# Routing divided in two halves and the shared expert begun on the first half's norm, in a fused ViT tower kernel

## The chip, the cores and the metric

The kernel runs on one core of a Trainium2 chip. The metric is the device time of one execution in microseconds. The kernel before was run three times: 373.65, 376.08 and 376.28 us.

## What is computed

16 images of 96x96 pixels become 36 patch tokens each and one class token: 592 tokens of width 256. Then come two blocks. The reference, cut to the block that the change touches:

```python
h = tok(x, ...)                                   # (16, 37, 256)
h = h + attn(layernorm(h), ...)                   # 16 heads of 64, relative bias, softmax
h = h + ffn(layernorm(h), ...)                    # below
h = h + scan_attn(layernorm(h), ...)              # second block
h = h + channel_mix(layernorm(h), ...)
...
def ffn(x, router_w, w_gate, w_up, w_down, sw_gate, sw_up, sw_down):
    logits = x_flat @ router_w.T                  # 7 experts
    top_vals, top_idx = top_k(logits, 2)
    top_w = softmax(top_vals)
    combine = sum(one_hot(top_idx, 7) * top_w[..., None], axis=1)
    routed_out = swiglu(x_flat, w_gate, w_up, w_down)      # hidden width 1024
    mixed = einsum("end,ne->nd", routed_out, combine)
    shared_out = swiglu(x_flat, sw_gate, sw_up, sw_down)   # one shared expert
    return mixed + mean(shared_out, axis=0)
```

All of it is float32. The kernel makes each float32 product as three products of a high and a low part (`three`): high x high, high x low, low x high.

## The kernel before

The state `hT` lies transposed in SBUF: two blocks `m` of 128 channels by 592 tokens. The tokens are cut into two halves `c` of 296 columns. TensorE (PE) makes the products, ScalarE (ACT) the activations and the high parts (`piece_high`, `high`, `shared_high`), VectorE (DVE) the gate products and most low parts (`sub` at L859, called by `piece_low`, `low` and `shared_low`), GpSimd (POOL) the remaining low parts of weights (`half_low` L386, `down_low` L391) and the scatters, SyncE (SP) the loads. Each engine has its program written out by hand, in one block for each; the order in the code is the order on the engine, and semaphores tie the engines together. The weights of an expert come in five pieces: gate and up in halves `g0`, `u0`, `g1`, `u1`, and `dn`. Expert 0 is the shared one, 1 to 7 the routed ones.

Layer norm of a half is a chain over three engines: `mean` (PE, L1362, two float32 products with a matrix of ones), `centre` (DVE, L891), `square` (ACT, L536), `variance` (PE, L1369), `root` (ACT, L541 and L543: logarithm and exponential), `normal` (DVE, L896), `high` (ACT, L547), `low` (DVE, L859). The order around the change is this.

- PE ends the attention's output projection (`output`, with the first half's mean and variance between its products), then makes the second half's mean and variance, and then begins the shared expert. ACT and DVE make in that time the high and low parts of the shared expert's weights, POOL the low parts of `u1` and `dn`.
- The shared expert runs over 12 units `u` here (the last 4 come behind the routed experts). A unit is one block of 128 hidden channels for one half: 12 products of 296 columns (`gate_up`), Silu on ACT (L639), the gate product on DVE (L1074), high part on ACT (L646), low part on DVE, and two units later six down products on PE (`down`). Units 0 to 7 belong to the first half, 8 to 11 to the second.
- Routing lies between the units. `logits` (PE, L1542) stands behind unit 1 and waits for the second half's norm. `rank_experts` (DVE) compares the seven logits of every token of five tiles of 128 tokens pair by pair. `positions` (PE, L1565) gives each token its place in its expert's list: for each tile one triangular product and products with ones for all tiles before it, 20 in all. `rows` turns places into row numbers. `turn_tokens` (PE, L1555) turns the normed tokens, `tokens_copy` (ACT, L653) takes them over, and POOL scatters each tile twice by row number into `expert_rows` in DRAM (L425, ten scatters). SP waits for all of them and loads the rows of expert 1 (L346) and of the others (L348). `turn_rows(1)` in unit 11 turns expert 1's rows for PE.
- In unit 6 ACT makes the exponentials of the shifted logits (L666), which `token_weights` (DVE) turns into weights. The exponential and Silu lie in different tables, so the engine loads one table ahead of it (ACT_TABLE_LOAD, L666) and the other behind it (L639).
- Then the seven routed experts follow, each with 256 gathered rows, some 18.5 us each by the chain.

## Time and profile before

| | us |
|---|---|
| three runs: lowest, median, highest | 373.65, 376.08, 376.28 |
| profiled execution, its own time | 373.84 |
| profiled execution, span of the core | 371.6 |
| PE busy in the span | 334.2 (90%) |
| DVE, ACT, POOL busy | 209.7, 194.0, 152.6 |

The rows below come from this one profiled execution. Times are microseconds from the start of the span. The span runs from the first to the last instruction; the execution's own time is 2.2 us longer. The granted clock is a share of TensorE's full 2.4 GHz.

### The profile page before, as it was taken

How to read it: one execution, taken by the hardware profiler on the slowest of the kernel's cores; microseconds unless marked ns; L12 is line 12 of the kernel's file. 1: busy time of each engine (PE TensorE's matmuls, PEld its weight loads, DVE VectorE, ACT ScalarE, POOL GpSimd, SP SyncE). 2: the span in 40 equal slices, each digit the busy share in tenths (PEclk: the TensorE clock that was granted, in tenths of full speed). 3: DMA queues.
4: the chain of work that ended last, by engine and by line, in shares of the span. 5: the costliest groups of instructions: out<-in, count | busy, mean ns of one | idle time of the engine just before them, and what ended most of it. 6: DMA issues, size and time to landing. Idle time of an engine off the chain costs nothing.

```text
span 371.6 us, 7692 instructions
## 1 busy us (share of the span) xinstructions
PE 334.2 (90%) x3284; PEld 309.9 (83%) x3284; DVE 209.7 (56%) x347; ACT 194.0 (52%) x322; POOL 152.6 (41%) x103
## 2 busy tenths in 40 slices
PE   7979999999999599779999999999999969578794
PEld 6957877899989399779999999999999969457694
DVE  2773233566536853155757574747474764637586
ACT  4662233756536633446566666666666554245491
POOL 3050021674422503732646464646464888100031
PEclk9998999999999799969999999999999998879899
DMA  8836440003002520282664656464648232100001
GB/s 294 342 113 192 118 178 2 4 10 109 4 2 78 191 89 28 101 268 71 198 199 165 211 163 207 161 220 155 207 163 284 85 113 59 30 3 0 2 1 65
DMA packets 31426, 45.40 MB, mean 122 GB/s; under 512 B 1714, under 2 KB 20226, under 8 KB 31260
## 3 DMA queue, kind: packets, MB, share of 16 engines
q1 hardware_dynamic: 28140, 39.84, 32.2%
q0 software_dynamic: 1200, 3.03, 2.7%
q10 hardware_dynamic: 2048, 1.99, 1.8%
q8 instruction: 27, 0.44, 0.5%
q14 instruction: 11, 0.09, 0.1%
HBM read 38.80 MB, written 5.88 MB: 120 GB/s over the span
## 4 chain that ended last, share of the span: by engine, by line
PE 73%; DVE 10%; ACT 6%; issue 5%; DMA 2%; another core or an unknown queue 1%; SPq 1%; POOL 0%; DVEq 0%; ACTq 0%
PE ps L1337 21%; PE ps L1339 19%; PE ps L1338 19%; PE ps L1468 2%; PE ps L1495 2%; PE ps L1369 2%; DMA w_stage<-in_w_v 2%; PE ps L1362 2%; DVE xn_lo L859 2%; DVE c_region L859 2%; PE ps L1453 1%; DVE w_lo L859 1%; DVE x_centred L891 1%; DVE v_region L1269 1%
## 5 line engine op out<-in xcount | busy, mean ns | idle before, releaser
L1337 PE MATMUL ps<-c_region,w_hi 128*128 128x256 f32 (+2 forms) x320 | 95.0, 297 | 7.6 <-DVE c_region L859 7.2
L1338 PE MATMUL ps<-c_region,w_hi 128*128 128x256 f32 (+2 forms) x320 | 92.3, 289 | 0.0
L1339 PE MATMUL ps<-c_region,w_lo 128*128 128x256 f32 (+2 forms) x320 | 92.3, 288 | 0.0
L386 POOL TENSOR_TENSOR w_lo<-w_stage,w_hi 128x1024 fp32r<-128x1024 f32 x16 | 47.7, 2981 | 58.3 <-ACT w_hi L619 58.3
L1337 PEld LDWEIGHTS ps<-c_region,w_hi 128*128 128x128 f32 x320 | 61.5, 192 | 9.6 <-DVE c_region L859 8.9
L1338 PEld LDWEIGHTS ps<-c_region,w_hi 128*128 128x128 f32 x320 | 61.5, 192 | 0.1
L1339 PEld LDWEIGHTS ps<-c_region,w_lo 128*128 128x128 f32 x320 | 61.4, 192 | 0.0
L859 DVE TENSOR_TENSOR c_region<-s_region,c_region 128x512 fp32r<-128x512 f32 (+1 forms) x44 | 49.0, 1114 | 16.1 <-ACT c_region L743 15.4
L1337 PE MATMUL ps<-xn_hi,w_hi 128*128 128x296 f32 x152 | 49.3, 324 | 6.1 <-issue 3.4
L619 ACT ACTIVATE w_hi<-w_stage 128x1024 fp32r<-128x1024 f32 (+1 forms) x43 | 51.6, 1209 | 4.1 <-DVE v_region L1189 3.4
L1338 PE MATMUL ps<-xn_lo,w_hi 128*128 128x296 f32 x152 | 47.2, 310 | 0.0
L1339 PE MATMUL ps<-xn_hi,w_lo 128*128 128x296 f32 x152 | 47.1, 310 | 0.0
L391 POOL TENSOR_TENSOR w_lo<-w_stage,w_hi 128x2048 fp32r<-128x2048 f32 (+1 forms) x9 | 39.3, 4371 | 13.5 <-ACT w_hi L619 11.5
L1337 PEld LDWEIGHTS ps<-xn_hi,w_hi 128*128 128x128 f32 x152 | 30.6, 201 | 7.4 <-issue 7.2
L1337 PE MATMUL ps<-w_hi,c_region 128*128 128x256 f32 x112 | 32.1, 287 | 3.5 <-issue 3.5
L403 POOL TENSOR_TENSOR s_region<-s_region,softmax_stats 101x296 f32<-101x296 f32 x16 | 11.1, 692 | 52.0 <-DVE softmax_stats L941 52.0
L1338 PE MATMUL ps<-w_lo,c_region 128*128 128x256 f32 x112 | 31.7, 283 | 0.0
L1339 PE MATMUL ps<-w_hi,c_region 128*128 128x256 f32 x112 | 31.7, 283 | 0.0
L1159 DVE TENSOR_TENSOR s_region<-s_region,ps 128x512 f32<-128x512 f32 x28 | 19.0, 679 | 21.2 <-ACT s_region L738 21.2
L743 ACT ACTIVATE c_region<-s_region 128x512 fp32r<-128x512 f32 x28 | 17.7, 633 | 24.8 <-DVE s_region L1159 22.9
L1338 PEld LDWEIGHTS ps<-xn_lo,w_hi 128*128 128x128 f32 x152 | 30.6, 201 | 0.0
L1339 PEld LDWEIGHTS ps<-xn_hi,w_lo 128*128 128x128 f32 x152 | 30.4, 200 | 0.0
(164 smaller groups left out, 621.7 us busy)
## 6 DMA issues: line engine op xcount, KB each, us to landing
w_stage<-in_w_gate SPq DMA_DIRECT2D x17, 512.0 KB, 3.8
w_stage<-in_w_up SPq DMA_DIRECT2D x17, 512.0 KB, 4.5
w_stage<-in_w_down SPq DMA_DIRECT2D x8, 1024.0 KB
expert_rows<-zeros SPq DMA_DIRECT2D x1, 1792.0 KB, 14.1
expert_out<-v_region ACTq DMA_DIRECT2D x7, 256.0 KB, 4.8
v_region<-in_patches SPq DMA_DIRECT2D x3, 576.0 KB, 6.0
v_region<-expert_rows SPq DMA_DIRECT2D x1, 1536.0 KB, 7.5
v_region<-in_w_l SPq DMA_DIRECT2D x1, 1280.0 KB, 6.9
```

Source lines behind the costliest of these rows:

```text
L386: g.tensor_tensor(piece(wl, n), piece(ws, n), piece(wh, n).bitcast(F32), ALU.subtract).then_inc(lo_e[n], 1)
L391: g.tensor_tensor(piece(wl, "dn", rows), piece(ws, "dn", rows), piece(wh, "dn", rows).bitcast(F32), ALU.subtract).then_inc(lo_e["dn"], 1)
L403: g.tensor_tensor(sc, sc, pat(stat[0:QR, :], (t % 3) * 24, [1, 8], [0, T]), ALU.subtract).then_inc(s["shifted"], 1)
L619: a.activation(piece(wh, n, rows), piece(ws, n, rows), ACT.Copy).then_inc(hi_e[n], 1)
L743: a.activation(gh_h[:, i * G:(i + 1) * G], prod_g[:, (i % 2) * G:(i % 2 + 1) * G], ACT.Copy).then_inc(s["g_hi"], 1)
L859: return v.tensor_tensor(o, x, hi.bitcast(F32), ALU.subtract)
L1159: v.tensor_tensor(pat(prod_g, (i % 2) * G, [SLOTS, 2], [1, SLOTS]), pat(silu_g, (i % 2) * G, [SLOTS, 2], [1, SLOTS]), pat(bank(2 * (i % 2) ...
L1337: mm(o, a_h, b_h, start=start, stop=False)
L1338: mm(o, a_h, b_l, start=False, stop=False)
L1339: return mm(o, a_l, b_h, start=False, stop=stop)
L1362: w = mm(bank(2 * c, NC), ones[:], hT[:, k * N + c * NC:k * N + (c + 1) * NC], start=(k == 0), stop=(k == KD - 1))
L1369: w = mm(bank(var_bank(L, c), NC), ones[:], sq[:, k * N + c * NC:k * N + (c + 1) * NC], start=(k == 0), stop=(k == KD - 1))
```

## The change

It does the following.

- Routing is divided: tiles 0 and 1 (`TA` = 2, all in the first half) and tiles 2 to 4. Each part has its logits, ranking, positions and rows. The two parts use PSUM banks 7 and 6.
- The shared expert's first unit needs only the first half's norm. The second half's mean stands behind unit 0 on PE, its variance behind unit 1, its square, root and high part in units 0, 1 and 2 on ACT, its other steps in units 0 to 2 on DVE. Between `root` and the next Silu ACT switches tables twice.
- Positions are two float32 products for each part: the triangular matrix gives the place inside a tile, the matrix of ones each tile's total. DVE copies the totals into a small table and scans it (`tensor_tensor_scan`) for the first place of each tile.
- The exponentials for the weights move from unit 6 to the end of expert 1, `token_weights` and `choice_weights` to expert 2.
- The shared down weights are made in two halves, high on ACT, low on DVE; POOL makes the low parts of `u0` and of `u1`, the second half of `u1` after unit 0's gate product.
- The third turning of tokens uses the bank of the second and waits for its copy (`xt_ok` 2).
- The routing constants become columns of `const` (277 to 622 columns); their own load on ACT's queue goes. SP loads `u0` ahead of `g1`.

The core of the diff:

```diff
@@ block.sync
             load("g0", 0)
-            load("g1", 0)
             sp.wait_ge(w_lo[1], 1)
             sp.wait_ge(s["up_lo"], 1)
             load("u0", 0)
+            load("g1", 0)
             load("u1", 0)
@@ block.gpsimd
-            half_low("u1", 0)
-            down_low(0)
-            pool.wait_ge(s["d_zero"], 16)
-            pool.wait_ge(s["rows_set"], 1)
+            half_low("u0", 0)
+            pool.wait_ge(hi_e["u1"], 1)
+            for k in range(KD):
+                if k == 1:
+                    pool.wait_ge(s["gate_mul"], 1)
+                r = slice(W1 + k * HID + HID // 2, W1 + (k + 1) * HID)
+                w = g.tensor_tensor(wl[:, r], ws[:, r], wh[:, r].bitcast(F32), ALU.subtract)
+            w.then_inc(lo_e["u1"], 1)
+            pool.wait_ge(s["d_zero"], 48)
             for t in range(TT):
+                pool.wait_ge(s["rows_set"], 1 if t < TA else 2)
                 pool.wait_ge(s["xt_ok"], (1, 1, 2, 2, 3)[t])
@@ block.scalar
-            piece_high("g0", 0)
-            piece_high("g1", 0)
+            for n in ("g0", "u0", "u1", "g1"):
+                piece_high(n, 0)
             square(1, 0)
-            piece_high("u0", 0)
-            piece_high("u1", 0)
             root(1, 0)
+            high(1, 0)
+            preload(ACT.Silu, 7)
             act.wait_ge(s["wo_mm"], 4)
-            piece_high("dn", 0)
-            high(1, 0)
-            square(1, 1)
-            root(1, 1)
-            preload(ACT.Silu, 7)
+            shared_down_high(0, s["dn0_hi"])
...
             for u in range(FRONT):
                 silu(0, u)
                 if u == 0:
+                    shared_high(0)
+                    square(1, 1)
+                    tokens_copy(0)
+                if u == 1:
+                    log_exp_tables()
+                    root(1, 1)
+                    shared_high(1)
+                    preload(ACT.Silu, 7)
+                if u == 2:
                     high(1, 1)
-                if u >= 1:
-                    shared_high(u - 1)
-                if u in (2, 3, 5):
-                    tokens_copy((2, 3, 5).index(u))
-                if u == 6:
-                    act.wait_ge(s["rt_shift"], 1)
-                    a.activation(route[:, 80:115], route[:, 80:115], ACT.Exp).then_inc(s["rt_exp"], 1)
+                    shared_down_high(1, hi_e["dn"])
+                if u >= 2:
+                    shared_high(u)
+                if u in (5, 6):
+                    tokens_copy(u - 4)
...
+                    if e == 1:
+                        weight_exponentials()
                     act.wait_ge(s["g_y"], e)
@@ block.vector
             add_attention(0)
             add_attention(1)
+            piece_low("g0", 0)
             centre(1, 0)
-            piece_low("g0", 0)
+            add_attention(2)
             piece_low("g1", 0)
-            piece_low("u0", 0)
-            add_attention(2)
-            add_attention(3)
             normal(1, 0)
-            centre(1, 1)
             low(1, 0)
...
+            def rows(i, t0, t1):
...
+                dve.wait_ge(s["pos_mm"], i)
+                link(v.tensor_copy(pat(tot, 1 + t0, [1, n], [TT + 1, E]),
+                                   pat(bank(route_bank(t0)), TOT0 + t0 * 8, [8, n], [1, E])))
+                link(v.tensor_tensor_scan(first, rcb[:, RB_KEEP:RB], tot, 0.0, ALU.mult, ALU.add))
...
+            take_logits(1, 0, TA)
+            add_attention(3)
+            rank_experts(0, TA)
             for u in range(FRONT):
...
                 if u == 0:
+                    centre(1, 1)
+                    shared_down_low(0, s["dn0_hi"], s["dn0_lo"])
+                if u == 1:
+                    shared_low(0)
+                    rows(1, 0, TA)
+                    normal(1, 1)
+                    shared_low(1)
+                if u == 2:
                     low(1, 1)
-                if u >= 1:
-                    shared_low(u - 1)
-                if u == 1:
-                    rank_experts()
+                if u == 5:
+                    rows(2, TA, TT)
+                if u >= 2:
+                    shared_low(u)
+                if u == 3:
+                    take_logits(2, TA, TT)
+                    rank_experts(TA, TT)
+                if u == 4:
+                    shared_down_low(1, hi_e["dn"], lo_e["dn"])
@@ block.tensor
-            output(1, 1, 0, HP // 2)
+            output(1, 1, 0, 1)
             variance(1, 0)
-            output(1, 1, HP // 2, HP)
-            mean(1, 1)
-            variance(1, 1)
+            output(1, 1, 1, HP)
...
-            def positions():
-
-                pe.wait_ge(s["sel_set"], 2)
-                for t in range(TT + 1):
-                    o = bank(6, 8, POS0 + t * 8) if t < TT else bank(6, 8, CNT0)
-                    for j in range(min(t + 1, TT)):
-                        w = mm(o, tri_r if j == t else one_r, sel_r[:, j * 8:(j + 1) * 8],
-                               start=(j == 0), stop=(j == min(t, TT - 1)))
+            def positions(t0, t1, chosen):
+
+                pe.wait_ge(s["sel_set"], chosen)
+                b, r = route_bank(t0), slice(t0 * 8, t1 * 8)
+                for o, c_ in ((POS0, RB_TRI), (TOT0, RB_ONES)):
+                    w = mm(bank(b, (t1 - t0) * 8, o + t0 * 8), rcb[:, c_:c_ + P], sel[:, r], start=True, stop=True)
                 w.then_inc(s["pos_mm"], 1)
...
+            logits(0, TA, 3)
             half_ready(0, 0)
             pe.wait_ge(s["ln_lo"], 3)
             gate_up(0, 0)
+            mean(1, 1)
+            turn_tokens(0)
             gate_up(0, 1)
-            logits()
+            positions(0, TA, 2)
+            variance(1, 1)
```

**What the order shows.** Three places are given, of the kernel before and of the changed one apart. A row is one instruction or several alike (x3), with the tensor that it writes, the tensors that it reads, its size and the semaphores that it waits for.

PE, from the last product of the attention's output projection to the shared expert's first, before:

```order
L1339 MATMUL ps<-c_region,w_lo 128x296
L1362 MATMUL ps<-hT,ones_over_d 128x296 [waits h_ready]
L1362 MATMUL ps<-hT,ones_over_d 128x296
L1369 MATMUL ps<-x_squared,ones_over_d 128x296 [waits ln_sq]
L1369 MATMUL ps<-x_squared,ones_over_d 128x296
L1337 MATMUL ps<-xn_hi,w_hi 128x296 [waits ln_lo,lo_u0,lo_g0]
```

and in the changed kernel:

```order
L1400 MATMUL ps<-c_region,w_lo 128x296
L1601 MATMUL ps<-params,xn_f 128x7 [waits ln_xn]
L1601 MATMUL ps<-params,xn_f 128x7 x3
L1398 MATMUL ps<-xn_hi,w_hi 128x296 [waits ln_lo,lo_u0,lo_g0]
L1399 MATMUL ps<-xn_lo,w_hi 128x296
```

The second half's mean and variance have left this place, and four logit products (tiles 0 and 1) stand there.

ACT, units 6 and 7 of the shared expert before, with the exponential (`s_region` 128x35) between two table loads:

```order
L646 ACTIVATE c_region<-s_region 128x296 [waits dn_mm,gate_mul]
L666 ACT_TABLE_LOAD
L666 ACTIVATE s_region<-s_region 128x35 [waits rt_shift]
L639 ACT_TABLE_LOAD [waits gate_mul]
L639 ACTIVATE s_region<-ps 128x296 [waits gu_mm]
```

and units 1 and 2 in the changed kernel:

```order
L655 ACTIVATE s_region<-ps 128x296 [waits gu_mm]
L527 ACT_TABLE_LOAD
L557 ACTIVATE rstd<-ps,eps 128x296 [waits ln_var]
L559 ACTIVATE rstd<-rstd 128x296 [waits ln_log]
L662 ACTIVATE c_region<-s_region 128x296 [waits gate_mul]
L548 ACT_TABLE_LOAD
L548 ACTIVATE small<-eps 128x1
L655 ACTIVATE s_region<-ps 128x296 [waits gate_mul,gu_mm]
```

The pair of table loads in the shared expert now encloses the second half's root, ahead of unit 2; the exponential's pair is in experts 1 and 2.

DVE, from the end of the rows (`count_i`) to unit 5's gate product and low part, before:

```order
L1044 CAST count_i<-v_region 128x1
L1074 TENSOR_TENSOR s_region<-s_region,ps 128x296 [waits hid_lo,hid_hi,silu_ok]
L859 TENSOR_TENSOR c_region<-s_region,c_region 128x296 [waits hid_hi]
L1074 TENSOR_TENSOR s_region<-s_region,ps 128x296 [waits hid_lo,hid_hi,silu_ok]
L859 TENSOR_TENSOR c_region<-s_region,c_region 128x296 [waits dn_mm,hid_hi]
```

and from the end of the second ranking to unit 5's gate product in the changed kernel:

```order
L1043 TENSOR_REDUCE s_region<-s_region 128x21 [waits dve_chain]
L1044 TENSOR_SCALAR s_region<-s_region 128x21 [waits dve_chain]
L1045 TENSOR_TENSOR s_region<-s_region,consts 128x3x7 [waits dve_chain]
L1120 TENSOR_TENSOR s_region<-s_region,ps 128x296 [waits hid_lo,hid_hi,silu_ok]
L889 TENSOR_TENSOR c_region<-s_region,c_region 128x296 [waits dn_mm,hid_hi]
L889 TENSOR_TENSOR w_lo<-w_stage,w_hi 128x1024 [waits hi_dn]
L1120 TENSOR_TENSOR s_region<-s_region,ps 128x296 [waits hid_lo,hid_hi,silu_ok]
```

Between unit 3 and unit 5 DVE now has the ranking of tiles 2 to 4 and half of the down weights' low part.

## Rows read from the trace of the kernel before

**Rows 1.** The stretches by engine (us; busy and count; granted clock; DMA).

```profile
125.00:131.40 6.40, 4.46 (x15) 3.49 (x15) 4.28 (x5) 2.44 (x4) 2.56 (x1) 0.50 0.41 131
...
158.70:165.60 6.90, 5.25 (x21) 5.25 (x22) 3.45 (x10) 3.70 (x8) 2.87 (x1) 0.52 0.85 276
```

**Rows 2.** Chain that ended last, first norm half to shared expert (start, us, what).

```profile
120.88 0.15 PE ps L1339
121.06 0.48 DVE hT L968
121.58 1.28 PE ps L1362 x4
...
128.33 0.58 PE ps L1337
```

**Rows 3.** Timeline of DVE over the same stretch.

```profile
123.59 4.60 DVE L859 TENSOR_TENSOR xn_lo<-xn_f,xn_hi 128x592 fp32r<-128x592 f32 x1
```

**Rows 4.** Timeline of POOL, weight low part and last scatter.

```profile
123.05 4.51 POOL L391 TENSOR_TENSOR w_lo<-w_stage,w_hi 128x2048 fp32r<-128x2048 f32 x1 [1.45 <-ACT w_hi L619]
...
156.32 0.91 POOL L425 DMA_INDIRECT expert_rows<-v_region,row_i  x1 [0.30 <-issue]
```

**Rows 5.** Chain that ended last, the pause in the shared expert.

```profile
153.18 1.28 ACT L639
154.47 4.51 another core or an unknown queue
...
159.83 0.47 DVE c_region L859
...
160.96 0.25 PE ps L1338
```

**Rows 6.** Timeline of SP, first load behind the scatters.

```profile
158.63 0.37 SPq L346 DMA_DIRECT2D v_region<-expert_rows  x1
```

**Rows 7.** Timeline of PE, an f32 pair of products inside the output projection.

```profile
113.98 1.16 PE L1362 MATMUL ps<-hT,ones_over_d 128*128 128x296 f32 x4
114.75 0.52 PE L1337 MATMUL ps<-c_region,w_hi 128*128 128x296 f32 x1
```

**Rows 8.** Chain that ended last, logits and positions.

```profile
133.53 2.40 PE ps L1542 x20
...
140.57 2.13 PE ps L1565 x20
```

**Rows 9.** Timeline of ACT, switch back to Silu.

```profile
127.44 1.28 ACT L532 ACT_TABLE_LOAD   x1
128.73 0.20 ACT L532 ACTIVATE small<-eps 128x1 f32<-128x1 f32 x1
```

**Rows 10.** DVE groups by form between 100 and 175 us (busy, mean ns).

```profile
L859 DVE TENSOR_TENSOR w_lo<-w_stage,w_hi 128x1024 fp32r<-128x1024 f32 x5 | 5.9, 1221 | 0.2 <-ACT w_hi L619 0.2
...
L1006 DVE TENSOR_TENSOR s_region<-s_region 128x245 f32<-128x245 f32 x1 | 0.4, 416 | 0.0
...
L1013 DVE TENSOR_TENSOR c_region<-s_region,v_region 128x35 fp32r<-128x35 f32 x1 | 0.2, 196 | 0.0
```

**Rows 11.** Timeline of PE, seventh unit, end of the second pause, turning of gathered rows.

```profile
148.95 0.38 PE L1337 MATMUL ps<-xn_hi,w_hi 128*128 128x296 f32 x1
...
160.35 0.61 PE L1337 MATMUL ps<-c_region,w_hi 128*128 128x296 f32 x1 [4.62 <-DVE c_region L859]
...
170.25 0.60 PE L1579 MATMUL ps<-consts,v_region 128*128 128x128 f32 x4
```

**Rows 12.** DMA issues: KB each, median us to landing.

```profile
v_region<-expert_rows SPq DMA_DIRECT2D x1, 256.0 KB, 2.8
consts<-in_const SPq DMA_DIRECT2D x1, 138.5 KB, 6.6
```

**Rows 13.** Page, part 2: GB/s in 40 slices of 9.3 us.

```profile
GB/s 294 342 113 192 118 178 2 4 10 109 4 2 78 191 89 28 101 268 71 198 199 165 211 163 207 161 220 155 207 163 284 85 113 59 30 3 0 2 1 65
```

**Rows 14.** Chain that ended last, at the start.

```profile
5.45 7.96 DMA w_stage<-in_w_v
```

202 lines of the change are left out of this document (116 added, 86 removed).

## The prediction

> **What bounds the kernel now.** I read the page first. TensorE (PE) is busy 90% of the span, so time can only be won where PE stands still, where it runs at the lower clock, or where it does work that can be left out. The second view was the row of granted clocks and then the stretches by engine: between 125 and 131.4 us and between 158.7 and 165.6 us the granted clock is 0.50 and 0.52, that is 1.2 GHz where the neighbours have 2.4 [rows 1]. Both stretches lie in the part that the change rewrites, the norm before the expert stage and the shared expert, and each follows a pause of PE. The third view was the chain of waits around both.
>
> First pause: the last product of the attention output ends at about 121.0, the second half's mean follows at 121.58, and the first product of the shared expert starts at 128.33 [rows 2]. What it waits for is DVE's low part of the first half's norm: a 128x592 subtraction that took 4.60 us [rows 3]. POOL worked on a 128x2048 weight low part from 123.05 to 127.56 [rows 4], and the subtraction ended 0.6 us after that. So DVE's subtraction of two SBUF operands stood still behind POOL's.
>
> Second pause: ACT loads the Silu table at 153.18 after the routing's exponential, and its next instruction starts only at 159.0 [rows 5]; PE resumes at 160.35 after 4.62 us without work [rows 11]. The profile names no engine for these 4.51 us. They end just where the last scatter has landed: the load that waits for all scatters is issued at 158.63 [rows 6]. Behind each pause the products are 0.25 us apart [rows 5] where they were 0.15 apart before it [rows 2].
>
> **The change part by part.** All times are on the axis of the profiled execution (span 371.6, own time 373.84).
>
> (a) First pause. The shared expert no longer waits for the second half. Its inputs are the first half's norm and the low parts of g0 and u0. The first half's own variance stands nine products earlier, so ACT's root can start some 1.3 us earlier. POOL now has u0 (from ACT's second high part, about 113.7, for 2.9 us) and half of u1, and the down weights have left it; it waits at u1's second half until unit 0's gate product. So no POOL work lies beside DVE's low part of the norm, which should take 0.8 and be done by about 121.7. PE meanwhile does the logits of tiles 0 and 1: 4 of 10 products, 20 records in 2.40 [rows 8], so 8 records of 0.12, 1.0 us. The first shared product starts at about 122.1 instead of 128.33: 6.2 us. If DVE's g1 low part falls behind POOL's u1 piece, it ends about 119.4 and the norm still comes in time; without that cover the price would be some 1 us.
>
> (b) The lower clock behind it. The first unit's 12 products ran 0.25 apart instead of 0.14: 12 x 0.11 = 1.3 us.
>
> (c) PE's own work. The remaining 12 logit records cost 1.4 in the place of 2.4: 1.0 us. The positions, 20 records in 2.13 [rows 8], become two f32 products in each half. No row shows this form; the nearest is the logits, an f32 call with two records, so 8 records of 0.12: 1.0 us, saving 1.2. Bounds: four records (0.5) and, if the 16 or 24 columns cost as the f32 products of 296 do (0.77 for two, [rows 7]), 1.6. Against this, the second half's mean and variance are now between products. A mean of this kind holds the next product up by 0.77, which is itself 0.1 to 0.2 slower [rows 7]: 1.0 each, together minus 2.0.
>
> (d) A new wait. The third turning of tokens now uses the bank of the second and waits for ACT's copy of it. That copy stands behind unit 5's gate on ACT, and this behind a queue on DVE: after unit 3 come the take-over and ranking of tiles 2 to 4 (five operations between 0.20 and 0.42, [rows 10], so about 0.35 each, and three of 0.2: 2.4 us), unit 4's two operations, and 1.2 for the second half of the down weights [rows 10], then unit 5. Followed, unit 5's gate product ends at 141.5, the copy at 142.5, and PE arrives at 140.6. That is 2.0 us; bounds are 0 (the handshakes overlap better) and 4 (each of some ten handshakes is 0.2 longer). Queued behind PE's waiting instruction is unit 6, and nobody else waits. The clock fell in the trace behind pauses of more than twice that; I leave it at the upper level and take 2.0.
>
> From (a) to (d): 6.2 + 1.3 + 1.0 + 1.2 - 2.0 - 2.0 = 5.7 us. Unit 6, at 148.95 before [rows 11], should start at about 143.2.
>
> (e) Second pause. The exponential and the switch back to Silu have left the shared expert. If the pause goes with them, PE gains its 4.6 us [rows 11], and the 21 products to 165.6 that ran at half clock, 21 x 0.11 = 2.3: 6.9 us. What is late next is the gathered rows. The scatters of tiles 0 and 1 start at about 130.5, well covered. The other six wait for the rows of the second half, about 143.1 in my hand trace; at 0.91 + 0.30 each [rows 4] they end at 150.6, land by 152, and the load takes 2.8 [rows 12]: 154.9. PE turns these rows at 170.25 before [rows 11], now at 157.6. Slack 2.7 us. The whole cover is that; if the scatters start 4 us later, 1.3 is lost.
>
> (f) The exponential in expert 1 stands on ACT where it waits for the expert's down products anyway. The switch back delays expert 2's first Silu by 1.28 [rows 9]; PE wants the product of that Silu only after the 24 products of its second step. Nothing, bounds 0 and 1.3. Token weights on DVE have the same kind of cover: nothing.
>
> (g) The start. The constants grow from 277 to 622 columns, 138.5 KB [rows 12] to 311, ahead of w_v, whose load ends the wait at 13.4 us and is on the chain [rows 14]. 172 KB at the 294 to 342 GB/s of the first slices [rows 13] are 0.5 to 0.6 us, at most; I take minus 0.5. The routing constants' own load behind the attention goes, hidden before.
>
> Sum: 5.7 + 6.9 - 0.5 = 12.1; 373.84 - 12.1 = 361.7. The three runs have a median of 376.08, 2.24 above the profiled execution. I carry a quarter, 0.6, since a pause that varies would be the first thing to differ between runs and it is among what goes: 362.3.
>
> A rule of the Trainium skill speaks against the three added switches. Here the row is first: the table load at 127.44 took 1.28 and the activation stands right behind it, at 128.73 [rows 9]. ScalarE: Activation LUTs, section What ACT_TABLE_LOAD costs, adds about 1.38 us of drain to each load. By that rule unit 1's two switches make ACT 2.8 us later, which the new wait of (d) passes on: 364.5 plus 0.6. It is a rival below, priced there by rows.
>
> **The rivals.**
>
> R1, the pause stays. ACT would not be held by the table but by something that the scatters hold, and it is freed when they land. For: it ends with them [rows 5, 6], and the switch at 127.44, with no scatter under way, had none [rows 9]. Against: ACT ran on through the first scatters, and only the instruction behind a switch was held. In the changed kernel ACT at unit 7 (147.2) would stand until about 152.0; PE has work to 150.4 and resumes at about 153: 2.6, plus 2.3 for the clock: 4.9. 362.3 + 4.9 = 367.2.
>
> R2, ACT's switches cost more than their 1.28 (a drain, or longer handshakes on ACT and DVE): up to 2.8 more at unit 1, passed on in full by (d): 365.1. For: the long hand-over at 154.47. Against: 128.73. The skill's drain would be this case.
>
> R3, slower. Every switch back to Silu has the pause of the second one: 4.6 and 2.3 of clock, 6.9 us. There are now three (before unit 0, in unit 1, before expert 2). It decides from two on: 362.3 + 13.8 = 376.1, and with three 383.0. Against: of two such switches in the trace one had no pause.
>
> R4, the first half cannot start early: DVE's g1 low part and the norm behind it stand behind POOL's u0 and u1 pieces (as [rows 3, 4] show for another pair), and the chain of ACT and DVE in units 0 to 2 starves PE for the 5.7 us of (a) to (d). Then only the second pause goes: 362.3 + 5.7 = 368.0. Against: the wait for unit 0's gate product keeps POOL off most of it.
>
> **How the numbers follow.** My forecast 0.62, R1 0.18, R2 0.08, R4 0.08, R3 0.04. The forecast's own spread is the bounds of (c), (d) and (e), about 359 to 365, and up to 2.2 for the offset of the median. R1, R2 and R4 reach 368. Range 358 to 368. A measurement of this kernel tells about 1% from no change, 3.8 us: below 372.3 is faster. All cases but R3 are below it; two of its switches end as no change, three as slower. With a little for what I have not seen: faster 0.93, same 0.04, slower 0.03.
>
> **What would show it.** Right: the first shared product about 1 us after the attention output; the low part of the norm under 1 us; no clock of 0.5 between 120 and 160; a short wait of PE at the turning of two tiles behind unit 5; the load behind the scatters issued near 152; expert 1 about 12 us earlier. (e) falls if ACT shows one idle time of several us without an engine's name while scatters run. (a) falls if a DVE subtraction of several us stands before unit 0. A total above 370 would mean that both gains were given back.

## The result and the profile after

The changed kernel took 364.03 us (median of five runs, 363.31 to 365.81), the kernel before, run beside it, 375.86 (five runs). The ratio is 0.973, with a 95% interval from 0.969 to 0.976: faster. Here and below a ratio leaves out executions over 1.5% slower than the fastest of their kernel, a median does not. The forecast was 362.3 with a range of 358 to 368. The profiled execution is the slowest of the five: its own time is 365.81, its span 363.8. From its page, the engines' totals and the row of granted clocks in 40 slices of 9.1 us:

```profile
PE 332.2 (91%) x3272; PEld 307.1 (84%) x3272; DVE 214.3 (59%) x366; ACT 196.5 (54%) x326; POOL 150.4 (41%) x104
...
PEclk9988999999999999999999999999999989769898
```

The two stretches at lower clock of [rows 1], around 125 and 160 us, are gone; what is left stands at the start and in the tail. The timeline of PE, at the places that the prediction spoke of (start, duration, idle time before and what ended it):

```profile
122.58 0.30 PE L1400 MATMUL ps<-c_region,w_lo 128*128 128x296 f32 x1
122.71 0.95 PE L1601 MATMUL ps<-params,xn_f 128*128 128x7 f32 x8
123.54 0.37 PE L1398 MATMUL ps<-xn_hi,w_hi 128*128 128x296 f32 x1
...
128.67 1.24 PE L1430 MATMUL ps<-x_squared,ones_over_d 128*128 128x296 f32 x4
129.53 0.52 PE L1398 MATMUL ps<-xn_hi,w_hi 128*128 128x296 f32 x1
...
143.27 0.44 PE L1614 MATMUL ps<-consts,xn_f 128*128 128x128 f32 x2 [1.34 <-ACT v_region L669]
143.46 0.38 PE L1398 MATMUL ps<-xn_hi,w_hi 128*128 128x296 f32 x1
...
158.72 0.63 PE L1636 MATMUL ps<-consts,v_region 128*128 128x128 f32 x4 [0.77 <-DVE s_region L1120]
...
161.72 0.40 PE L1398 MATMUL ps<-c_region,w_hi 128*128 128x296 f32 x1 [0.69 <-DVE c_region L889]
```

The row at 122.71 (the first eight logit records) stands right behind the attention's last product, which starts at 122.58; the first shared product follows at 123.54, 0.96 behind the attention's last. Before, that distance was 7.61: the first shared product started at 128.33 [rows 2] and the attention's last one here:

```profile
120.72 0.30 PE L1339 MATMUL ps<-c_region,w_lo 128*128 128x296 f32 x1
```

The second half's variance (128.67) holds up the next product until 129.53. PE waits 1.34 at the third turning, and 0.77 and 0.69 in units 10 and 11. It never stands for the 4.6 us of [rows 11].

The norm's low part on DVE, and the second table load on ACT with the activation behind it:

```profile
122.61 0.78 DVE L889 TENSOR_TENSOR xn_lo<-xn_f,xn_hi 128x592 fp32r<-128x592 f32 x1 [0.76 <-ACT xn_hi L563]
```

```profile
128.94 1.28 ACT L527 ACT_TABLE_LOAD   x1
130.24 0.51 ACT L557 ACTIVATE rstd<-ps,eps 128x296 f32<-128x296 f32 x1
```

The subtraction takes 0.78 us instead of the 4.60 of [rows 3]. The switch takes 1.28, as in [rows 9], and the activation stands right behind it. Now ACT around the last scatters (POOL issues the last one at 150.25), and SP's load that waits for all of them:

```profile
149.15 1.04 ACT L633 ACTIVATE w_hi<-w_stage 128x1024 fp32r<-128x1024 f32 x1
152.59 0.42 ACT L655 ACTIVATE s_region<-ps 128x296 f32<-128x296 f32 x1 [2.39 <-remote]
```

```profile
152.55 0.37 SPq L357 DMA_DIRECT2D v_region<-expert_rows  x1
```

This is the row that the prediction named as evidence against its term (e). ACT's Silu of unit 8 starts at 152.59 after 2.39 us without work, no engine is named, no table is loaded there, and it starts when the scatters have landed (152.55), as in [rows 5, 6]. PE had ended unit 8 at about 150.3.

Two places give time back. One is expert 2. The rows of PE are the first down product of experts 1, 2 and 3 (175.68, 194.20, 214.76) and a wait ahead of the third; then the same three products before:

```profile
175.68 0.35 PE L1398 MATMUL ps<-w_hi,c_region 128*128 128x256 f32 x1 [0.64 <-issue]
...
194.20 0.35 PE L1398 MATMUL ps<-w_hi,c_region 128*128 128x256 f32 x1 [0.59 <-issue]
...
210.99 0.39 PE L1398 MATMUL ps<-c_region,w_hi 128*128 128x256 f32 x1 [1.45 <-DVE s_region L1212]
...
214.76 0.35 PE L1398 MATMUL ps<-w_hi,c_region 128*128 128x256 f32 x1 [0.64 <-issue]
```

```profile
186.37 0.35 PE L1337 MATMUL ps<-w_hi,c_region 128*128 128x256 f32 x1 [0.64 <-issue]
...
204.86 0.36 PE L1337 MATMUL ps<-w_hi,c_region 128*128 128x256 f32 x1 [0.57 <-issue]
...
223.36 0.36 PE L1337 MATMUL ps<-w_hi,c_region 128*128 128x256 f32 x1 [0.57 <-issue]
```

Before, they are 18.5 apart; after, 18.52 and then 20.56, with a wait of 1.45 for DVE's gate product between them. The other is the clock at the start. Stretches by engine of the changed kernel (granted clock is the column behind POOL):

```profile
core 0: us, PE busy (x) PEld busy (x) DVE busy (x) ACT busy (x) POOL busy (x), PEclk, DMA share, GB/s
19.00:21.00 2.00, 0.47 (x1) 0.50 (x2) 2.00 (x5) 1.18 (x1) 2.00 (x1) 0.83 0.76 201
21.00:23.00 2.00, 2.00 (x5) 1.35 (x4) 0.35 (x2) 0.73 (x1) 1.93 (x2) 0.50 0.91 322
23.00:25.00 2.00, 1.82 (x6) 1.01 (x5) 1.27 (x2) 0.70 (x1) 1.16 (x1) 0.82 0.00 1
```

Before, the clock was 1.00 there and fell to 0.66 at 28 to 32 us. In this execution it fell twice: again at 28 to 36 us, to 0.82 and 0.75. The first fall is common: of the ten profiles of the changed kernel and its variants it stands in seven, and not in `weights_early`, `exp_in_unit6` and `all_three`; of the four of the kernel before and its variants in one (`before_copy_for_exp`). Whether the change makes it more frequent, so few profiles don't show. The changed kernel's repetition and its variants without added products have the attention's last product at 120.07 to 121.25 us, this one at 122.58 and the kernel before at 120.72: most of the loss at the start belongs to the single execution.

The balance of the two profiled executions, by PE's rows: minus 1.86 at the end of the attention (0.35 of it the later start on w_v), plus 7.35 to unit 6 (28.23 us before, 20.88 after, counted from the attention's last product), plus 5.20 from there to expert 1's start (37.42 and 32.22), minus 2.06 in expert 2, minus about 0.9 in the tail, at lower clock (0.66 in the 15 us from 310, 0.77 in the 15 from 319 before). That is 7.7 of the spans' difference of 7.8.

### The profile page after: what moved, and what is told of

The parts are those of the page before. It is cut to its first block, busy times and chain, and to the rows that moved or that the text cites. A ratio compares the mean times of both kernels' runs of the same rounds, so it can differ in the third digit from the quotient of the medians.

```text
span 363.8 us, 7696 instructions
## 1 busy us (share of the span) xinstructions
PE 332.2 (91%) x3272; PEld 307.1 (84%) x3272; DVE 214.3 (59%) x366; ACT 196.5 (54%) x326; POOL 150.4 (41%) x104
## 4 chain that ended last, share of the span: by engine, by line
PE 62%; DVE 16%; ACT 10%; issue 7%; DMA 2%; SPq 1%; another core or an unknown queue 1%; ACTq 0%; POOL 0%; DVEq 0%
PE ps L1398 17%; PE ps L1400 15%; PE ps L1399 15%; DVE c_region L889 4%; PE ps L1423 3%; PE ps L1430 2%; PE ps L1529 2%; PE ps L1556 2%; DMA w_stage<-in_w_v 2%; DVE w_lo L889 2%; DVE s_region L1212 1%; PE ps L1514 1%; ACT w_hi L633 1%; ACT L548 1%; ACT c_region L770 1%
## 5 line engine op out<-in xcount | busy, mean ns | idle before, releaser
L633 ACT ACTIVATE w_hi<-w_stage 128x1024 fp32r<-128x1024 f32 (+1 forms) x42 | 49.6, 1192 | 5.5 <-DVE v_region L1246 5.5
L1398 PE MATMUL ps<-xn_hi,w_hi 128*128 128x296 f32 x152 | 48.1, 316 | 4.1 <-issue 3.3
L1399 PE MATMUL ps<-xn_lo,w_hi 128*128 128x296 f32 x152 | 46.0, 303 | 0.0
L1400 PE MATMUL ps<-xn_hi,w_lo 128*128 128x296 f32 x152 | 45.9, 302 | 0.0
L402 POOL TENSOR_TENSOR w_lo<-w_stage,w_hi 128x2048 fp32r<-128x2048 f32 (+1 forms) x8 | 34.8, 4348 | 14.1 <-ACT w_hi L633 14.1
L1398 PEld LDWEIGHTS ps<-xn_hi,w_hi 128*128 128x128 f32 x152 | 29.4, 193 | 4.9 <-issue 4.4
L889 DVE TENSOR_TENSOR w_lo<-w_stage,w_hi 128x1024 fp32r<-128x1024 f32 (+1 forms) x22 | 28.8, 1307 | 2.7 <-ACT w_hi L532 2.4
L1399 PEld LDWEIGHTS ps<-xn_lo,w_hi 128*128 128x128 f32 x152 | 29.3, 192 | 0.1
```

Source lines behind the costliest of these rows:

```text
L402: g.tensor_tensor(piece(wl, "dn", rows), piece(ws, "dn", rows), piece(wh, "dn", rows).bitcast(F32), ALU.subtract).then_inc(lo_e["dn"], 1)
L633: a.activation(piece(wh, n, rows), piece(ws, n, rows), ACT.Copy).then_inc(hi_e[n], 1)
L889: return v.tensor_tensor(o, x, hi.bitcast(F32), ALU.subtract)
L1398: mm(o, a_h, b_h, start=start, stop=False)
L1399: mm(o, a_h, b_l, start=False, stop=False)
L1400: return mm(o, a_l, b_h, start=False, stop=stop)
```

## The experiments

Three theories were open. T: a table switch is held while scatters run (the prediction's). S or C: something of the scatters holds the units' hand-over, with or without a switch. F, formed after the first four runs: PE's instruction packets among the scatters are the cause. Beside these, the loss in expert 2 and the terms (a), (d) and (g) were tested one at a time. Times of different groups were not taken side by side; the ratio to the kernel before, run beside them, is the safer number. Of a single profile, the distances between two of PE's rows tell more than the total, since the clock at the start and in the tail differs from one execution to the next.

### The changed kernel once more

> The changed kernel as it is, beside the three others of this job, so that they are compared on one chip. Expected: 364.0 us within 1 us; if the 1.5 us that the profiled execution lost to a lower clock at 20 to 25 us is a matter of the single execution, this profile has the first mean at 2.3 us for 8 records instead of 3.8.

365.02 us (362.76 to 365.35), ratio 0.974 [0.968, 0.981]. The first mean's eight records took 3.53, so the clock fell early here too, against what I expected. It did not fall a second time, and the attention's last product stands at 120.94. PE's waits are the same: 1.34, 0.19, 0.77, 0.69, and 1.43 in expert 2.

### Where the token weights stand

```diff
-                    if e == 2:
-                        token_weights()
-                        dve.wait_ge(s["comb_set"], 2)
-                        choice_weights()
                     dve.wait_ge(s["g_y"], e)
...
                     v.tensor_copy(y_s[:, o:o + D], bank(5, D)).then_inc(s["y_ok"], 1)
+                    if e == 1:
+                        token_weights()
+                        dve.wait_ge(s["comb_set"], 2)
+                        choice_weights()
```

> Only the place of the token weights on DVE changes: from ahead of expert 2's output copy to behind expert 1's, where DVE stands idle from 182.1 to 186.5 and POOL until 184.6. Theory: expert 2 is 20.56 us long instead of 18.5 because a 128x35 product took 2.40 us beside POOL's 128x1024 low part and the output copy, the next expert's down weights and the first gate product stand behind it; then expert 2 falls to 18.5, the time by 2.06 to 362.0, and the product takes 0.2. Rival: the loss is the switch back to Silu (1.28) at the head of expert 2; then expert 2 stays above 20 us and the time at 364.

360.08 us (358.83 to 362.61), ratio 0.965 [0.958, 0.972]. The reading starts with the changed kernel's chain of waits in expert 2 and POOL's row beside its first line:

```profile
198.81 2.33 DVE s_region L1055
...
202.40 0.34 DVE v_region L1246
...
203.18 1.92 ACT w_hi L633
...
207.00 3.34 DVE c_region L889
...
210.99 0.39 PE ps L1398
```

```profile
197.98 3.10 POOL L397 TENSOR_TENSOR w_lo<-w_stage,w_hi 128x1024 fp32r<-128x1024 f32 x1 [2.84 <-ACT w_hi L633]
```

A product of 35 columns held DVE for 2.33 us, until POOL's subtraction ended at 201.1 (the row itself is 2.40 long). Behind it stood the output copy, behind that ACT's high part of the down weights (203.18), then Silu and the gate product, and at 207.00 DVE was held once more, for 3.34, by POOL's next piece. PE got the result at 210.99. With the weights moved:

```profile
179.63 0.57 DVE L1055 TENSOR_TENSOR s_region<-s_region 128x35 f32<-128x35 f32 x1
```

```profile
191.79 0.36 PE L1398 MATMUL ps<-w_hi,c_region 128*128 128x256 f32 x1 [0.59 <-issue]
...
210.27 0.36 PE L1398 MATMUL ps<-w_hi,c_region 128*128 128x256 f32 x1 [0.55 <-issue]
```

The product takes 0.57, and from expert 2's first down product to expert 3's it is 18.48. The table load at its head is still there, so the rival (the switch) is out; `exp_in_unit6` below shows the same from the other side, with no table load there and still 20.57. The median is 4.9 us below the run above, and 2.06 of them are this edit. The profiles differ besides by 0.9 at unit 6, ahead of the edit, and by 3.5 behind expert 7's first down product, with a mean granted clock of 0.987 here and 0.971 above.

### The exponentials back in unit 6

```diff
                 if u in (5, 6):
                     tokens_copy(u - 4)
+                if u == 6:
+                    act.wait_ge(s["rt_shift"], 1)
+                    a.activation(ex, ex, ACT.Exp).then_inc(s["rt_exp"], 1)
...
-                    if e == 1:
-                        weight_exponentials()
```

> The exponentials go back to unit 6 of the shared expert on ACT, with their two table loads, all else as changed. Theory T (a table switch under way while scatters run is held until they have landed): ACT's Silu of unit 7 starts at 152.5 instead of 147.9, PE stands about 2.5 us and runs at the lower clock behind it, 2.3: the time rises by 3 to 5 us, less up to 1.3 for the switch that leaves expert 2. Rival S (something of the scatters holds ACT at some instruction, with or without a switch, as at 150.2 to 152.6): ACT's Silu of unit 7 is 2.6 us late by the two loads and the exponential, the pause stays about 2.4 and ends with the scatters; the time rises by 0 to 2 us.

364.34 us (363.34 to 365.45), ratio 0.975 [0.969, 0.982]: no difference to the changed kernel. From unit 6 to expert 1's first down product it is 32.28 us, against 32.33 in the changed kernel's run beside it. ACT:

```profile
147.14 1.28 ACT L655 ACT_TABLE_LOAD   x1
148.43 0.42 ACT L655 ACTIVATE s_region<-ps 128x296 f32<-128x296 f32 x1
...
151.20 0.42 ACT L655 ACTIVATE s_region<-ps 128x296 f32<-128x296 f32 x1 [0.43 <-remote]
```

Silu of unit 7 stands right behind the table load, at 148.43, with five of the six scatters issued and one to come. The pause is only before unit 8, and it ends at 151.20, when the scatters have landed (their load is issued at 151.08). Theory T is wrong.

### The kernel before with a copy for the exponential

```diff
-                    a.activation(route[:, 80:115], route[:, 80:115], ACT.Exp).then_inc(s["rt_exp"], 1)
+                    a.activation(route[:, 80:115], route[:, 80:115], ACT.Copy, bias=2.0).then_inc(s["rt_exp"], 1)
```

> The kernel before with a copy (plus 2.0) in the place of the exponential in unit 6, so that ACT loads no table there; the routed experts' weights are not the reference's, all work and waits are. Theory of the prediction (the switch is held, so the pause goes with it): the pause of 4.6 us and the 2.3 for the clock go, the time falls by 6 to 7 to about 368.5. Theory F: PE's counts are held all the same, ACT waits for them instead of behind the switch, PE's pause stays between 4 and 4.7, the time within 1 of before.

374.74 us (ten runs, 373.56 to 378.85), ratio 1.001 [0.997, 1.005]. Without either table load ACT idles 6.32 us instead of 4.54, to the same moment:

```profile
152.47 0.22 ACT L666 ACTIVATE s_region<-s_region 128x35 f32<-128x35 f32 x1
159.01 0.42 ACT L639 ACTIVATE s_region<-ps 128x296 f32<-128x296 f32 x1 [6.32 <-remote]
```

PE resumes at 160.36 after 4.48 us; before it was 160.35 after 4.62. From unit 6 to expert 1 it is 37.41 us, before 37.42. The second pause never had to do with the table.

What ACT waits for shows in the trace's times of semaphore updates: PE's count of finished units. In the kernel before, unit 7's last product ends at 153.27, its count is updated at 158.98, 5.7 us late, and that of unit 8 0.20 us later. In the changed kernel unit 8's is due at 150.28 and comes at 152.56, and unit 9's, on time, at 152.78. PE works on; its message is late.

### PE's instruction packets moved

```diff
             keep_clock(15)
+            small(10)
...
+            small(10)
             pe.wait_ge(s["cls_set"], 1)
             norm(0)
```

(`small(n)` makes n products of one column on zeros. In the kernel before: `small(8)` at these two places, `small(7)` and `small(8)` ahead of and behind the second half's variance.)

> The changed kernel with 20 one-column float32 products on zeros added for PE, 10 at the start and 10 ahead of the first mean, where PE is idle: some 80 instructions, which moves PE's 16 KB instruction packets about 5 us ahead, the one at 147.4 to about 142.5, before the second wave of scatters (144.0). Theory F: the counts of units 8 and 9 come on time, ACT's pause of 2.4 us is gone, PE's waits of 0.2, 0.77 and 0.69 at units 10 and 11 shrink, the way from unit 6 to expert 1 is about 1.5 us shorter; at the start up to 1 us is lost, so the time falls by 0.5 to 1.5. Rival C: the pause stays as it was, the way from unit 6 to expert 1 stays 30.7 us from turning to turning, and the time rises by up to 1.

> The kernel before, its exponential with both table loads in unit 6 left as it is, with 31 one-column products on zeros where PE is idle (8 at the start, 8 ahead of the first mean, 15 around the second half's variance): some 124 instructions, which moves PE's packet from 151.4 to about 143.7, ahead of the scatters (145.0 on). Theory F: the pause of 4.6 us with its lower clock (2.3) goes although the table switch stays; ACT's Silu behind the switch stands right behind it or behind PE's unit; the time falls by 5 to 7 us, to about 368, less up to 1 for the start. Rival T (the switch or the scatters make the pause): the pause stays at 4 us or more, the time at 375 within 1.5.

369.04 us (ratio 0.987 [0.982, 0.991]) and 378.47 (1.012 [1.006, 1.018]). The packets did move ahead: the DMA view has PE's starting between 143 and 144 and between 148 and 149 us, with the scatters issued from 147.53 and from 149.87 on. The pauses stayed, and so did the way from unit 6 to expert 1: 32.26 us (32.33 in the repeated run) and 37.43 (37.42 before). ACT before unit 8 of the changed kernel, and PE in the kernel before:

```profile
156.19 0.42 ACT L655 ACTIVATE s_region<-ps 128x296 f32<-128x296 f32 x1 [2.44 <-remote]
```

```profile
165.66 0.62 PE L1337 MATMUL ps<-c_region,w_hi 128*128 128x296 f32 x1 [4.48 <-DVE c_region L859]
```

Theory F is wrong as well, for PE's packets. The trace has smaller instruction packets (8 KB, queue 14) among the scatters too, and no run moved those. My estimate for the start was wrong too: ten float32 products of one column, 20 records, took 2.29 us at each of the two places and did not fit in the idle time; the third turning stands at 146.83, 5.2 us later than in the repeated run.

```profile
20.45 2.29 PE L1411 MATMUL ps<-zeros 128*128 128x1 f32 x20
```

### The last six scatters later

```diff
                 pool.wait_ge(s["rows_set"], 1 if t < TA else 2)
+                if t == TA:
+                    pool.wait_ge(s["gate_mul"], 9)
```

> The changed kernel with its last six scatters held until unit 8's gate product. In the traces so far PE's count of finished units comes 2.3 us late for unit 8 (due 150.3, seen 152.56) and 5.5 us late in the kernel before (due 153.4, seen 158.98), each time with a 16 KB packet of instructions for PE (queue 8) read among the scatters, at 147.4 and 151.4. Theory F (the late counts need both, that packet and the scatters behind or beside it): with the packet at 147.4 and the scatters from 150.8 on, ACT's Silu of unit 8 follows unit 8 at 150.3 without a pause, and none comes later. Rival C (the end of a row of scatters alone holds the counts): the hold of 2 us or more stands again before the scatters' end, at 156 to 159. The rows come 6 us later in both, so PE waits for them at the turning of rows and the time is 2 to 5 us longer.

369.43 us (one run). Silu of units 8, 9 and 10 followed PE at once. Only that of unit 11 came late: its last product ended at 155.74, the count came at 157.29, 1.6 us later.

```profile
148.40 0.42 ACT L657 ACTIVATE s_region<-ps 128x296 f32<-128x296 f32 x1
...
157.32 0.42 ACT L657 ACTIVATE s_region<-ps 128x296 f32<-128x296 f32 x1 [2.57 <-remote]
```

```profile
150.06 1.07 POOL L444 DMA_INDIRECT expert_rows<-v_region,row_i  x1 [14.71 <-DVE s_region L1122]
...
156.44 0.91 POOL L444 DMA_INDIRECT expert_rows<-v_region,row_i  x1 [0.30 <-issue]
```

The hold went with the scatters, from unit 8 to unit 11, near the end of their row. So rival C has it, though with a shorter hold than its 2 us: the place in the program does not matter. The total is higher for another reason, expected in both theories: PE waits 5.99 us for the rows at their turning, and from unit 6 to expert 1 it is 36.57 us instead of 32.3.

### All ten scatters in one row

```diff
-                pool.wait_ge(s["rows_set"], 1 if t < TA else 2)
+                pool.wait_ge(s["rows_set"], 2)
```

> The changed kernel with all ten scatters behind the second half's rows, in one row of 12.7 us from 144.0 to 156.6 as in the kernel before; no other edit. Theory H (PE's counts are held while scatters land, longer the longer the row: 5.5 us with ten, 2.3 with six): a count of PE is held by 4 us or more to about 157.5, PE stands 3 to 5 us between units 9 and 11 and its clock falls behind the pause; besides that the rows land 6 us later, at about 161, which costs up to 3 in their place. The time rises by 5 to 8 to about 370. Rival: the hold does not depend on the length of the row and stays 2.3; then only the late rows cost, 2 to 4 us, and PE's one long wait is that for expert_rows at the turning.

368.54 us (364.56 to 371.45), ratio 0.979 [0.972, 0.987]. In the totals that overlaps the changed kernel's 0.974 [0.968, 0.981]; in the profile the way from unit 6 to expert 1 is 35.64 us against 32.33, 3.3 longer. ACT, then the stretches of PE:

```profile
157.69 0.42 ACT L655 ACTIVATE s_region<-ps 128x296 f32<-128x296 f32 x1 [4.86 <-remote]
```

```profile
153.00:155.00 2.00, 1.17 (x9) 1.11 (x9) 0.57 (x1) 0.00 (x0) 1.39 (x3) 1.00 0.19 66
155.00:157.00 2.00, 0.74 (x5) 0.41 (x3) 0.00 (x0) 0.00 (x0) 1.98 (x2) 1.00 0.28 82
157.00:159.00 2.00, 0.53 (x2) 0.35 (x2) 0.46 (x1) 0.78 (x3) 1.08 (x1) 0.77 0.32 100
159.00:162.00 3.00, 3.00 (x16) 3.00 (x16) 2.05 (x5) 0.97 (x4) 0.00 (x0) 0.58 1.01 348
```

PE started unit 9's last product at 151.06; its count, due at 151.4, came at 157.66 and unit 10's 0.21 later. PE worked 0.53 of the 2 us from 157, and its clock is 0.58 behind the pause. So the long hold and the pause with its lower clock are back with nothing but the row of ten. The way to expert 1 grew by less than the 5 to 8 expected; the late rows (load issued at 157.10 instead of 150.93) cost nothing of their own, since PE turns them at 161.67 without a wait.

The times of the updates show more than the one hold. Three counts here, due at 148.92, 149.74 and 151.36, come at 150.46, 154.05 and 157.66: 1.5, 4.3 and 6.3 late, one at a time, and those left follow the last of them within 0.3 us. The other rows of ten look alike: 1.1, 3.2 and 5.9 in `before_copy_for_exp` and `before_pool_held`, 1.2, 3.2 and 5.9 in `before_fetch_moved`, 2.3 and 5.7 in the kernel before. With six, `after_again` has 0.5, 3.3 and 2.5. It reads as if counts passed slowly during a row and a queue of them built up, so that a longer row ends with a longer hold; no run tests that alone. (Some updates are missing in the trace; those left are assigned in their order.)

### POOL held in the kernel before

```diff
             half_low("u1", 0)
+            pool.wait_ge(s["ln_lo"], 3)
             down_low(0)
```

> The kernel before with POOL's low part of the shared down weights held until DVE has made the low part of the first half's norm; that takes POOL's 4.51 us from beside DVE's 4.60. Theory (term a): the DVE subtraction takes 0.8, the first shared product starts about 0.8 + 0.9 behind the high part, at 124.5 to 125 instead of 128.33, but only when the second half's variance (124.4 to 126.4) is over, so at 126.5; POOL's piece ends at about 129.5 and the first down product waits for it and the reloads; the time falls by 1 to 3 us. Rival: DVE was slow for another reason, its subtraction stays above 3 us and the time at 375 within 1.5.

372.23 us (ten runs, 370.25 to 374.68), ratio 0.995 [0.991, 0.998]. DVE's norm of the first half (low part) and of the second half, and PE:

```profile
122.05 0.77 DVE L860 TENSOR_TENSOR xn_lo<-xn_f,xn_hi 128x592 fp32r<-128x592 f32 x1
...
125.29 2.88 DVE L897 TENSOR_TENSOR xn_f<-x_centred,rstd 128x592 f32<-128x592 f32 x1 [2.15 <-ACT rstd L544]
```

```profile
123.78 0.52 PE L1338 MATMUL ps<-xn_hi,w_hi 128*128 128x296 f32 x1
...
129.76 1.39 PE L1543 MATMUL ps<-params,xn_f 128*128 128x7 f32 x11 [2.35 <-DVE xn_lo L860]
```

The subtraction took 0.77 for 4.60, and the first shared product came 4.60 us behind the attention's last product instead of 7.61. That is 1.2 us earlier than I expected: the variance in front was done by then. But POOL's piece, now from 122.90, held the next DVE operation (2.88 for 0.79), and PE waited 2.35 for the second half's norm at the logits. Term (a) had the right cause. PE's way to unit 6 (from the attention's last product) is 27.50 us, 0.7 shorter than before. What this edit does not win is the time of the second half's mean and variance, which still stand in front.

### Copy, constants, and the three together

```diff
+                if u == 5:
+                    tokens_copy(1)
                 if u >= 2:
                     shared_high(u)
-                if u in (5, 6):
-                    tokens_copy(u - 4)
+                if u == 6:
+                    tokens_copy(2)
```

> On ACT the copy of the second turning stands ahead of unit 5's high part instead of behind it; ACT then has it by about 141.7 and PE, which comes at 141.8, does not wait at the third turning (1.34 us in the changed kernel). Theory: the wait is on the path and nothing is late behind it, the time falls by 1.3 to 362.7. Rival: the rows of the second half come from DVE's queue and the scatters end where they did, so that the pause of ACT at 150.2 and DVE's queue at units 10 and 11 take it up: the wait goes, the time stays within 0.4 of 364.0.

362.40 us (362.01 to 365.11), ratio 0.971 [0.964, 0.978]; the run of the changed kernel beside it 0.974. The wait at the third turning is gone and expert 1's first down product stands 1.74 us earlier than in that run (172.43 and 174.17), of which 0.2 is there already ahead of unit 5. Unit 8's count, due at 146.86, came at 149.33 here, 1.3 us ahead of the last landing, and only the next one waited for that (due 147.67, come 150.78); so nothing was given back. The totals alone do not tell the two apart.

```diff
-            sp.dma_start(cb[:], const).then_inc(s["d_const"], 16)
+            sp.dma_start(cb[:, 0:CB_R], const[:, 0:CB_R]).then_inc(s["d_const"], 16)
...
+            sp.dma_start(cb[:, CB_R:CB], const[:, CB_R:CB]).then_inc(s["d_const"], 16)
...
             def rank_experts(t0, t1):
+                dve.wait_ge(s["d_const"], 32)
```

> The changed kernel with the routing constants (345 columns) loaded behind w_q instead of ahead of w_v. Theory (term g): w_v lands 0.3 to 0.5 earlier, so that ACT's first high part of it starts at about 13.4 instead of 13.78 as in the kernel before, and all behind it with it. Rival: the load of w_v is bounded by its own queue, its start stays at 13.8.

361.73 us (one run, clock 0.985). ACT's first high part of w_v starts at 13.66, against 13.78 and 14.00 in two profiles of the changed kernel and 13.43 before. That start also varies with the work ahead of it; ACT's wait for the load is steadier: 1.42 before, 1.88 and 1.87 in the two profiles of the changed kernel, 1.38 here and 1.42 in `all_three`. By the wait the larger load costs some 0.45 us, and the edit takes it back. One run can't show that in the total.

> The changed kernel with three edits together: token weights behind expert 1's output copy (2.06 us), the second turning's copy ahead of unit 5's high part (1.34), the routing constants behind w_q (0.35). They stand in three places of the path that do not overlap, so I expect the sum, 3.7 us less than the changed kernel: 360.3 us, between 359 and 361.5, and a ratio to before of 0.961. If one gain is given back, it is that of the copy: then 361.6.

363.38 us (six runs, 358.26 to 368.22), ratio 0.962 [0.954, 0.969]. The ratio is near the 0.961 expected, but it rests on three of the six times; these scatter by 10 us, and the interval takes in the ratio of the token weights alone (0.965). In its profile the wait at the turning is gone, but PE stands later:

```profile
152.03 0.40 PE L1402 MATMUL ps<-xn_hi,w_hi 128*128 128x296 f32 x1 [1.58 <-DVE s_region L1124]
```

ACT's hold before unit 8 lasted 3.83 us here and ended at 151.06, with the scatters' landing (load at 151.00). PE reaches unit 6 1.5 us earlier than in the changed kernel, and the way from there to expert 1 is 33.72 us instead of 32.33. So the gain of the copy was given back, as the expectation's last sentence has it. Of the three edits only that of the token weights keeps its gain in every profile that has it (18.48 in expert 2 here too). The ratios of `weights_early` (0.965) and `all_three` (0.962) lie below the changed kernel's 0.973 and can't be told apart.

## Why the prediction was right, and where it was not

The total is right: 362.3 forecast, 364.03 measured; the gain was forecast at 13.8 us and measured at 11.8. It came out so in part by luck, since two errors cancel. The steps, by the profiled executions:

- (a) 6.2 forecast. The first shared product came 0.96 behind the attention's last product instead of 7.61: 6.65. The cause was tested alone: 0.77 for 4.60 without POOL (`before_pool_held`).
- (b) 1.3: the first unit's products are 0.14 apart. Right.
- (c) Logits 1.0 forecast, 1.15 measured (0.83 of them are in (a)'s place, 1.25 behind unit 3). Positions 1.2 forecast: 0.36 and 0.37 instead of 2.13, 1.4. Mean and variance in the stream minus 2.0: 1.00 and 0.86 and the slower products behind them, 2.1.
- (d) minus 2.0 forecast, 1.34 measured. The wait stood where it was said, on the copy behind the gate; the run with the copy ahead took it away.
- Up to unit 6 this makes 5.7 forecast and 7.35 measured; the terms as measured give 7.1.
- (e) 6.9 forecast, 5.2 measured: here the mechanism failed. The step was "the exponential and the switch back to Silu have left the shared expert. If the pause goes with them". The pause stayed without them (`before_copy_for_exp`) and did not come back with them (`exp_in_unit6`). What shortened it is the division of the scatters: the hold of the count that ACT waits for is 5.7 to 6.3 us with ten in a row (five profiles) and 2.3 in the changed kernel with six (1.6 to 3.8 over its variants). PE had work until 153.4, and only the queue behind it on DVE cost 0.1, 0.77 and 0.69. The 4.62 and the 2.3 for the clock did go; these 1.6 are the difference. Rival R1 was the nearest, something that the scatters hold, and it named the evidence, but its price, 4.9, assumed that ACT stands until the end from unit 7 on.
- (f) nothing forecast, 2.06 measured: the sentence "Token weights on DVE have the same kind of cover: nothing" failed. I had seen in [rows 3, 4] that POOL holds a DVE subtraction of two SBUF operands, and did not ask what POOL does at the new place. It was no matter of the operation's size.
- (g) minus 0.5 forecast, minus 0.45 measured by ACT's wait for the load.
- R2 and R3 did not happen. Behind the table loads at 122.60, 128.94, 131.59 and 184.53 the next activation stands 1.28 to 1.30 us later, and in `exp_in_unit6` also with scatters under way (147.14 to 148.43); ahead of each of the four ACT's previous instruction ends within 0.02 us. No pause, no drain. By the rule of the Trainium skill that the prediction cited (ScalarE: Activation LUTs, What ACT_TABLE_LOAD costs) each would have shown 1.38 more. The trace disagrees, and the measurement decides.

The sum to expert 1 was 12.6 forecast and 12.55 measured, by two errors that cancel: plus 1.65 up to unit 6, minus 1.7 behind it. Expert 2's 2.06 is about what separates 364.0 from 362.3. On the axis of the profiled executions, where the sum was made, 12.1 was forecast and 7.8 measured: 2.1 of the difference is expert 2, the rest the lower clock at the start and in the tail of an execution that was the slowest of its five.

Open: why PE's counts are held, and what lets one through. In most profiles the last held count came with the last landing (within 0.6 us); in `late_scatters` the only late one came 1.5 us ahead of it, and in `copy_before_high` the one that ACT waits for 1.3 us ahead. No run took the scatters away, none spread them apart, and none moved the 8 KB instruction packets.

## What to carry to other kernels

A pause for which the profile names no engine is not put down to the instruction in front of it: take that instruction out in a run of its own, before the change is priced on it. Here scatters issued by POOL in a long row delayed the messages of an engine that has nothing to do with them; a shorter row, with work of PE at hand beside its end, hid most of it. Before a small DVE operation is moved, look at what POOL does at the new place: the price here was the rest of POOL's instruction (2.33 us for 35 columns), where the product takes 0.57 without it.

## What the runs showed that I had not expected

- PE's semaphore updates came up to 6.3 us late while scatters were under way, one every 3.6 us in `ten_in_row`, and those left within 0.3 us behind the last landing; its products went on meanwhile.
- The DVE product of 35 columns took 2.40 us in one place and 0.57 in the other.
- A float32 product of one column took 0.11 us a record, nearly as much as one of seven (0.12 in [rows 8]); 20 records took 2.29.
- The lower clock at the start and in the tail differs from run to run. The mean granted clock ran from 0.964 to 0.975 over five runs of one kernel, and their spans from 363.8 to 361.3; the shortest span had the highest clock.
